# Perceiver block: who issues the rope weights' loads, and where the shift of the exponential is added

## The reference

```
c_q, c_kv = x @ Wq_down, x @ Wkv_down
q_c, k_c, v_c = (c_q @ Wq_up), (c_kv @ Wk_up), (c_kv @ Wv_up)   # 128 heads of 8
q_r = (x @ Wq_rope).reshape(b, s, 128, 64)                      # Wq_rope: 1024 x 8192
k_r = x @ Wk_rope                                               # one for all heads
scores = (q_c . k_c + q_r . k_r) / sqrt(8 + 64)
attn = softmax(scores);  out = attn @ v_c;  x = x + out @ Wo
```

## Time and profile before

| | us |
|---|---|
| median of 3 runs | 1018.04 |
| lowest, highest | 1012.54, 1018.87 |
| profiled execution, its own time | 1024.18 |
| its span, first to last instruction | 1022.4 |

### The profile page before, as it was taken

The page is one execution under the profiler, slowest core; times in us unless marked ns, Lnnn a source line. Parts: engine busy times, 40 slices in busy tenths (PEclk is TensorE's granted clock), DMA queues, the critical chain, the costliest instruction groups (busy, mean ns, idle before and its releaser), DMA issues. The chain is left out here.

```text
span 1022.4 us, 18954 instructions
## 1 busy us (share of the span) xinstructions
PE 911.0 (89%) x6771; PEld 833.2 (81%) x6771; DVE 738.3 (72%) x1150; ACT 614.2 (60%) x1015; POOL 432.6 (42%) x274
## 2 busy tenths in 40 slices
PE   5999999899978899999898999957489999499987
PEld 5998888688857799889898889846389999498986
DVE  6547666644556387788787888868888889778954
ACT  4514434645516388878787788755467787366652
POOL 0210000244425856564464555302076676165663
PEclk9999999999988999999999999958789999699989
DMA  7567667666653788766676767824033442224221
GB/s 276 226 202 272 228 237 267 250 269 268 220 150 107 230 249 258 199 196 171 176 213 179 210 177 209 279 63 171 16 128 121 164 164 83 83 84 165 85 80 42
DMA packets 90215, 183.20 MB, mean 179 GB/s; under 512 B 9600, under 2 KB 67744, under 8 KB 87584
## 3 DMA queue, kind: packets, MB, share of 16 engines
q1 hardware_dynamic: 89664, 182.22, 54.3%
q10 hardware_dynamic: 480, 0.03, 0.0%
HBM read 161.51 MB, written 11.53 MB: 169 GB/s over the span
## 5 line engine op out<-in xcount | busy, mean ns | idle before, releaser
L52 PE MATMUL bank<-act_all,W_all 128*128 128x256 f32 (+1 forms) x512 | 158.6, 310 | 10.9 <-POOL W_all L1598 7.9
L52 PE MATMUL bank<-act_all,wh 128*128 128x256 f32 x512 | 146.3, 286 | 1.8 <-PEq L857 1.7
L54 PE MATMUL bank<-act_all,W_all 128*128 128x256 f32 (+1 forms) x512 | 146.3, 286 | 0.0
L53 PE MATMUL bank<-act_all,wh 128*128 128x256 f32 x512 | 146.1, 285 | 0.0
L54 PE MATMUL bank<-act_all,wl 128*128 128x256 f32 x512 | 146.0, 285 | 0.0
L1318 DVE TENSOR_TENSOR pl<-bank,ph 128x512 f16<-128x512 f32 x128 | 88.3, 690 | 56.1 <-ACT ph L1272 55.3
L459 POOL TENSOR_TENSOR xa_WT_l<-ring,xa_WT_h 128x1024 fp32r<-128x1024 f32 x16 | 41.5, 2610 | 186.3 <-ACT xa_WT_h L454 186.3
L850 POOL TENSOR_TENSOR wl<-ring,wh 128x1024 fp32r<-128x1024 f32 x32 | 76.5, 2391 | 102.2 <-ACT wh L842 102.1
L1261 ACT ACTIVATE bank<-bank,exp_shift 128x512 f32<-128x512 f32 x128 | 84.5, 660 | 47.5 <-PE bank L1189 46.6
L1598 POOL TENSOR_TENSOR W_all<-rnd,W_all 128x512 fp32r<-128x512 f32 x72 | 92.8, 1301 | 46.2 <-ACT W_all L1524 39.1
L52 PEld LDWEIGHTS bank<-act_all,W_all 128*128 128x128 f32 x512 | 100.2, 196 | 13.4 <-POOL W_all L1598 10.1
(11 more groups left out here) (219 smaller groups left out, 2625.3 us busy)
## 6 DMA issues: line engine op xcount, KB each, us to landing
ring<-in_ctx_dram SPq DMA_DIRECT2D x16, 2048.0 KB, 8.0
ring<-in_L_attn_Wq_rope_dram SPq DMA_DIRECT2D x32, 1024.0 KB, 7.9
ring<-in_L_ffn_W_dram SPq DMA_DIRECT2D x16, 2048.0 KB, 7.6
panel<-in_L_ffn_W_dram SPq DMA_DIRECT2D x48, 512.0 KB, 4.3
qmix<-qrope SPq DMA_DIRECT2D x128, 64.0 KB, 2.6
w1p<-in_L_ffn_W_dram SPq DMA_DIRECT2D x16, 512.0 KB, 3.9
ring<-in_L_xattn_Wq_dram SPq DMA_DIRECT2D x2, 2048.0 KB, 11.7
ring<-in_L_xattn_Wk_dram SPq DMA_DIRECT2D x2, 2048.0 KB, 8.1
```

What stands on the lines that cost most here:

```text
L52: pe.matmul(out, lh, rh, start=start, stop=False, skip_group_check=True)
L53: pe.matmul(out, lh, rl, start=False, stop=False, skip_group_check=True)
L54: return pe.matmul(out, ll, rh, start=False, stop=stop, skip_group_check=True)
```

## The change

The loads of the rope weights and of Wo within the heads leave SP's program and go to ACT's. At the head of its iteration g, ahead of `high_w` of group g+3, ACT waits until POOL has split group g+2 and issues the load of group g+4 (before: SP, in its iteration g-1, last). Group 2's load is issued by ACT in iteration -2 instead of by SP at the block's start. Each load uses the same buffer, semaphore and pieces as before.

The shift 10 ln 2 is no longer the bias of exp. The copy of the maxima rows adds 10 ln 2 * sqrt(72) as an immediate bias, so that after the scale the exponent is the same. `exp_shift`, its memset on POOL and one count of `filled` go.

```diff
-            exp_shift = sb(ml, "exp_shift", [P, 1])
...
-                    pool.memset(exp_shift[:, :], SHIFT).then_inc(filled, 1)
-                    pool.wait_ge(filled, 3)
+                    pool.wait_ge(filled, 2)
...
-                    def next_w(g):
-
-                        sp.wait_ge(w_lo, (g - 1) * 2)
-                        load(sp, g % 2, rope_raw(g % 2), rope_t[:, :, g * GC:(g + 1) * GC])
-
...
-                    next_w(2)
                     for g in range(FIRST, NG + 1):
...
-                        if valid(g + 5):
-                            next_w(g + 5)
-                        elif g + 5 < NG + 2:
-                            b = (g + 5) % 2
-                            sp.wait_ge(w_lo, (g + 4) * 2)
-                            load(sp, b, raw(b), wo_t[:, CH * b:CH * b + CH, :])
...
+                    def load_w(g):
+
+                        if 2 <= g < NG + 2:
+                            b = g % 2
+                            act.wait_ge(w_lo, (g - 1) * 2)
+                            if valid(g):
+                                load(act, b, rope_raw(b), rope_t[:, :, g * GC:(g + 1) * GC])
+                            else:
+                                load(act, b, raw(b), wo_t[:, CH * b:CH * b + CH, :])
...
-                                       bank[2][0:GROUP, 0:T].unsqueeze(1).to_broadcast([GROUP, GROUP, T]), ACT.Copy).then_inc(m_row, 1)
+                                       bank[2][0:GROUP, 0:T].unsqueeze(1).to_broadcast([GROUP, GROUP, T]), ACT.Copy,
+                                       bias=SHIFT / RSQRT).then_inc(m_row, 1)
...
-                        act.activation(bank[5 + h % 2][:, :], bank[5 + h % 2][:, :], ACT.Exp, scale=RSQRT,
-                                       bias=exp_shift[:, 0:1]).then_inc(ex_ready, 1)
+                        act.activation(bank[5 + h % 2][:, :], bank[5 + h % 2][:, :], ACT.Exp, scale=RSQRT).then_inc(ex_ready, 1)
...
                     for g in range(FIRST, NG):
+                        load_w(g + 4)
                         next_w(g + 3)
```

## The result

The changed kernel took 1027.19 us, median of 9 runs (1022.22 to 1029.92); before took 1016.68 in the 9 runs beside it (1010.32 to 1027.45). The ratio is 1.011, 95% interval 1.0073 to 1.0147; it leaves out one slow run of before, of 1027.45 us. The profiled execution took 1029.92 us, span 1028.0, against 1024.18 and 1022.4. The forecast was 992 us, 26 us faster.

What follows compares the result with a forecast made beforehand. PE was taken as the bound, losing time to late duplicates. Gains of 15.1 + 5.7 + 2.5 + 3.3 + 1 = 27.6 us, less 1.6 us kept for late pairs, gave 26 us: 1018.0 to 992 us, range 984 to 1010.

Steps and rivals of the forecast that it cites:

- The bound and the wait: Middle of the heads: PE is the bound, idling 15.9 us before `scores_q`, mostly for duplicates landing late behind a weight load.
- 15.1 + 5.7 us: Middle of the heads: 15.1 us of PE waits at L1159 and 5.7 us of low clock after three waits come back.
- Nearer to the free case, since only single packets of the other queue come between: Duplicates' landing before L1159: about 3 us, between 2.0 with nothing in flight and 6.5 as before.
- nothing was in flight: At 505 us, one group after the late pair: the duplicates took 1.9 and 2.0 us with no transfer queued ahead.
- nothing comes back: Rival, chance 0.15: the same engines carry the packets, only SP's issue time is saved, so time stays at 1018 us.
- Group 1: Start of the heads: its 1.84 us wait and half a clock loss come back, put at 2.5 us.
- Last group: End of the heads: with its pair early, 3.3 us of its 4.80 us wait come back, then maxima rows are late.
- ACT pays the issue: ACT's iteration head: each load's issue costs ACT 0.59 us, hidden by 1.02 us of slack, so no cost.
- ACT held at its head: Rival, chance 0.07: issue and late landing add up ahead of `high_w`, making the kernel slower, 1032 us.
- Shift: Exp without its bias tile: 0 to 64 ns shorter, 64 taken, 0.26 us a group off ACT, hidden behind PE.
- Range and chances: Whole kernel: range 984 to 1010 us; forecast 0.61; faster 0.77, same 0.16, slower 0.07.
- the cases that give no gain or a loss: Two rivals left out of the range: time stays at 1018 us, chance 0.15, or slows to 1032 us, 0.07.

Runs made afterwards that it cites:

- e8: Before, with w1p loaded in 256 KB halves, one in every group, each with its own maximum on DVE: 1001.47 us, ratio 0.9841.
- e11: Before, with w1p in 256 KB halves, one per group, and the shift's move; loads stay on SP: 1000.46 us, ratio 0.9856.
- e12: The changed kernel, with w1p in 256 KB halves, one per group, and the loads of groups 2 to 8 on SP: 997.04 us, ratio to before 0.9826.
- e7: The changed kernel, with w1p issued on ACT's queue as well: 1020.73 us, ratio to before 1.0015.
- e10: Before, with SP's load of group 3 moved ahead of the first content stores and group 0's second duplicates, same queue: 1022.68 us, ratio 1.0083.
- e9: The changed kernel, with the loads of groups 2 and 3 alone back on SP: 1019.88 us, ratio to before 1.0011.
- e1: Before, with the shift's move alone, loads left on SP: 1016.46 us, ratio 0.9966.
- e5: Before, with w1p loaded only once and all 16 maxima taken from that tile, 15 transfers left out: 1002.89 us, ratio 0.9864.

## Why the prediction was wrong, step by step

*The bound and the wait.* Right. PE is the bound and loses its time before `scores_q`, for duplicates that land late. e8, e11 and e12 took the waits of the middle away. From group 5's copy to group 31's it takes 625.5 - 374.1 = 251.4 us in e8, 250.4 and 249.7 in the other two, against 272.7 before: 21 to 23 us, near the 15.1 + 5.7 us that the prediction put on them. A group is at 9.6 to 9.7 us, also as forecast. The end gave nothing there: the last group waits 0.5 us and less for its pair, but the group ahead of it now waits 2.2 to 3.5 us, and from group 31's copy to the span's end it is 375.2 to 376.1 us against 376.5.

*"Nearer to the free case, since only single packets of the other queue come between": 3 us for the landing.* This is the step that failed. It measured 5.6 us, as with the load in the same queue. The prediction took the pair of the earlier trace rows, late behind a load, as a matter of order in one queue. The trace fitted the other reading as well, load on the engines: in the middle of before every late pair came with the group whose load and `w1p` make 1.5 MB. The words "nothing was in flight" at 505 us stood in the text and were not used. In before the load of 485.27, behind `w1p`, runs until 495.6, past the late pair of 491; the next one, without `w1p`, is issued at 494.24 and lands 7.5 us later, at 501.7, ahead of the early pair of 505. Of the rivals "nothing comes back" was right for the middle. The Trainium skill, "DMA: Bandwidth & Descriptors" (section "Issuing engines are not separate DMA queues"), says just this, that only the time to initiate is saved; the landings in e7 and in the changed kernel agree with it. The section "Queues, rings and completion order" of the same page, by which the queues are served in turn, was read as a promise of early landing; e7 gives 5.2 us.

*Group 1, "half a clock loss, 2.5 us": the time of the issue.* This term failed too, by its sign. The prediction followed the load of a middle group only. ACT's issue there comes at nearly the same place as SP's: at 542.60, 1.65 us ahead of the copy of the high weights at 544.25 (ACT's timeline below), where SP's in before came 1.8 us ahead of it, at 508.88 for the copy at 510.64. In the first groups the place is another. There the pipeline is half empty, content stores share the engines, and a load now goes ahead of a pair instead of behind it. The start loses 6.7 us in the profiled execution; by the medians that one load costs some 8 to 10 us (e10, e9), of which the traces place only a part. Instead of the gain of 2.5 us there is this loss. (1.84 and half of 1.9 would also be 2.8, not 2.5.)

*Last group.* 3.3 us were to come back; the wait grew to 6.07 us instead. Half a Wo was in flight there as before, 13.7 us long (10.8 before), and the second duplicate took 8.7 us. The term assumed an early pair, and the pair was later than before.

*ACT pays the issue: 0.59 us, slack 1.02 us.* Too dear and harmless. The issue takes 374 ns and begins while the copy before it still runs:

```profile
542.59 0.60 ACT L1268 ACTIVATE ph<-bank 128x512 f16<-128x512 f32 x1
542.60 0.38 ACTq L124 DMA_DIRECT2D ring<-in_L_attn_Wq_rope_dram  x1
543.22 1.01 ACT L1248 ACTIVATE qmix<-bank 4x1024 fp32r<-4x1024 f32 x1
544.25 1.06 ACT L841 ACTIVATE wh<-ring 128x1024 fp32r<-128x1024 f32 x1
```

So the slower rival, ACT held at its head, had the right sign and the wrong place: ACT waited 0.9 us in all for a load before L841, once.

*Shift.* Right that it is off the path (e1). Its size was 76 ns, a little over the 64 that was the upper bound taken; the 93 ns of the Trainium skill, "ScalarE: Activation LUTs" (section "What ACT_TABLE_LOAD costs"), is further off.

*Range and chances.* 0.22 stood on the cases that give no gain or a loss, by the argument that the delay went with what was queued ahead. No row could tell queue order from engine load, and the start's overlap with the content stores was not priced at all.

## What to carry to other kernels

A small transfer that is late beside large ones may be late by what the DMA engines carry, as here, and not by its queue: moving the large ones to another queue left it late, leaving some out or spreading them over the groups made it early. Try that, or issue them behind it. A load moved to another engine's program moves in time too: compare its issue with each latency-bound transfer around it in the ramp of a pipeline, not only in the steady state. And where a wait appears in every second period, ask first what else has that period.

## What the runs showed that I had not expected

DVE's add of two float32 tiles in SBUF (L1037, 128x256) takes 415 ns alone and 2.5 us when it starts within POOL's subtraction. The Trainium skill, "SBUF — State Buffer" (terms), says that the two engines share a port pair which one holds for a whole instruction; the rows agree. Before, DVE and then POOL:

```profile
477.52 2.52 DVE L1037 TENSOR_TENSOR onat<-rows_q 128x256 f32<-128x256 f32 x1
```
```profile
477.36 2.40 POOL L850 TENSOR_TENSOR wl<-ring,wh 128x1024 fp32r<-128x1024 f32 x1 [2.98 <-ACT wh L842]
```

In before the six that fall in the middle take 2.50 to 2.52 us. In e8 DVE has maxima of half the length, the adds start 0.37 us ahead of POOL's subtraction instead of 0.16 us behind its start, and they take 412 to 417 ns. e5 keeps the long maximum: each of its six slow adds is followed, 3.1 to 3.2 us after its start, by a PE wait for DVE of 0.7 to 0.95 us. That this is why e8's groups (9.67 us) are shorter than e5's (9.94) was not tried by itself.
